# A graph network kernel: joining edge features and edge ends into rows in the first stage

## What is computed

```python
edge_index = jnp.stack([src, dst])
x = _layernorm(x + gat(x, edge_index, ...))        # three attention layers with 4 heads
x = _layernorm(x + gin(x, src, dst, ...))          # sum over neighbours, then an MLP
x = _layernorm(x + dot(x, ..., src, dst))          # dot-product attention
x = _layernorm(x + edge_net(x, edge_index, edge_attr_32, ...))
```

```python
msg = jax.nn.relu(x[src] + edge_attr @ We + be)
aggr = jax.ops.segment_sum(msg, dst, num_segments=x.shape[0])
```

## Time and profile before

| | us |
|---|---|
| median of 3 runs | 5863.4 (5854.73 to 5868.62) |
| the profiled execution, its own time | 5863.81 |
| its span in the trace | 5862.1 |
| busy PE, DVE, ACT, POOL | 3511.6, 3123.5, 2625.6, 3883.7 |

### The profile page before, as it was taken

One profiled execution on the slowest core, in us unless ns is written; L12 is line 12 of the kernel. 1 busy time (PEld: TensorE's weight loads), 2 busy tenths in 40 slices (PEclk: granted clock), 3 DMA queues, 4 the chain that ended last, 5 costly groups with the idle time before them and its releaser, 6 DMA issues. The chain is left out here.

```text
span 5862.1 us, 68109 instructions
## 1 busy us (share of the span) xinstructions
PE 3511.6 (60%) x25247; PEld 2219.0 (38%) x25248; DVE 3123.5 (53%) x3383; ACT 2625.6 (45%) x4143; POOL 3883.7 (66%) x3309
## 2 busy tenths in 40 slices
PE   3211222221034699988999889997868781667764
PEld 2211111111034455555555555554433330455542
DVE  3644555554369555445555455555579992333323
ACT  1000000000023689888888789894059891222211
POOL 1888888888884577666776578773020787777772
PEclk7555555555566899999999999998989995677765
DMA  8222222222279699757997479875542332332222
GB/s 296 20 18 20 20 18 10 1 1 0 9 251 361 169 195 199 161 115 150 195 193 156 103 164 201 184 153 152 178 166 79 109 130 74 110 81 74 75 53 24
DMA packets 427191, 683.75 MB, mean 117 GB/s; under 512 B 177678, under 2 KB 272397, under 8 KB 422768
## 3 DMA queue, kind: packets, MB, share of 16 engines
q0 software_dynamic: 236096, 287.22, 31.9%
q1 hardware_dynamic: 172432, 350.48, 17.8%
q10 hardware_dynamic: 18336, 41.70, 2.1%
HBM read 540.73 MB, written 138.43 MB: 116 GB/s over the span
## 5 line engine op out<-in xcount | busy, mean ns | idle before, releaser
L330 POOL DMA_INDIRECT counts<-plcell_add,plcell_slot x806 | 1253.9, 1556 | 385.4 <-issue 223.2
L1704 POOL DMA_INDIRECT emxg<-xtab,emsrc x856 | 944.0, 1103 | 448.4 <-issue 257.8
L714 ACT ACT_TABLE_LOAD x1 | 1.3, 1283 | 1613.2 <-PE mtps L702 1613.2
L377 PE MATMUL plpsR<-plpiece,plbefore 128*128 128x500 bf16 (+1 forms) x81 | 47.1, 582 | 813.8 <-DVE plranked L507 800.6
L422 DVE TENSOR_REDUCE plnlow<-plsame 128x13 f32<-128x1664 bf16 x62 | 117.0, 1888 | 661.6 <-DMA counts<-plcell_add,plcell_slot 661.5
L1788 PE MATMUL dotbanks<-emmsg,emsame 128*128 128x96 f32 x1712 | 316.3, 344 | 237.4 <-DVE emsame L1968 230.1
L1176 ACT ACTIVATE ga1prob<-ga1psE,ga1src_fifth 128x512 f32<-128x512 f32 (+1 forms) x700 | 407.2, 680 | 81.8 <-PE ga1psE L1281 79.1
L1176 ACT ACTIVATE ga2prob<-ga2psE,ga2src_fifth 128x512 f32<-128x512 f32 (+1 forms) x700 | 407.5, 683 | 77.0 <-PE ga2psE L1281 74.1
L1176 ACT ACTIVATE ga0prob<-ga0psE,ga0src_fifth 128x512 f32<-128x512 f32 (+1 forms) x700 | 407.1, 678 | 77.7 <-PE ga0psE L1281 74.7
L1788 PEld LDWEIGHTS dotbanks<-emmsg,emsame 128*128 128x128 f32 x1712 | 287.2, 250 | 382.2 <-issue 379.5
L1281 PE MATMUL ga0psE<-ident,ga0logit 128*128 128x128 f32 x2500 | 394.5, 288 | 55.8 <-DMA ga0logit<-log_counts 32.7
(11 more groups left out here) (403 smaller groups left out, 8577.9 us busy)
## 6 DMA issues: line engine op xcount, KB each, us to landing
ga0logit<-log_counts POOLq DMA_DIRECT2D x88, 512.0 KB
ga1logit<-log_counts POOLq DMA_DIRECT2D x88, 512.0 KB
ga2logit<-log_counts POOLq DMA_DIRECT2D x88, 512.0 KB
counts<-plzeros SPq DMA_DIRECT2D x32, 1250.0 KB, 32.7
mthalf<-counts SPq DMA_DIRECT2D x50, 800.0 KB
log_counts<-mtlogs SPq DMA_DIRECT2D x25, 1600.0 KB
ginhalf<-counts SPq DMA_DIRECT2D x50, 800.0 KB
dotlogs<-log_counts ACTq DMA_DIRECT2D x25, 1600.0 KB
```

The lines of the kernel that those rows point to most:

```text
L330: nc.gpsimd.indirect_dma_start(counts[w][:, :], bass.IndirectOffsetOnAxis(ap=cell_slot[:, g % 2, j:j + 1], axis=0), cell_add[:, g % 2, j:j ...
L377: nc.tensor.matmul(psR[:, f // RANK_BANK, 0:k * BINS], before[:], piece[:, n % 2, f:f + k, :].rearrange("p t b -> p (t b)"), start=True, s ...
L714: nc.scalar.activation(logs[:, n % OUTS, q, :], ps[:, u % 3, 0:BW], ACT.Ln, bias=tiny[:, 0:1], scale=math.e).then_inc(log_made, 1)
L1704: nc.gpsimd.indirect_dma_start(xg[:, h, t, :], None, xtab[:, :], bass.IndirectOffsetOnAxis(ap=src[:, g, t:t + 1], axis=0)).then_inc(gather ...
```

## The change

In `begin`:

- The 128 spare cells of both tables are zeroed ahead of the tables, from one partition into 256 contiguous bytes.
- A tile `whole` of 3 x 13 rows of 34 words a partition is cleared by DVE. After the 54 pieces of the unused pattern, SP loads the features of one group after the other into the first 32 words of its rows. ACT copies the ends behind them. SP stores the rows to a new DRAM tensor `edges["rows"]`, which takes the place of `edges["ends"]`. A group's turn comes at every second add of table 1.
- The column lists and the slots are stored behind that loop, and the stage ends after the last rows have landed.

In `edge_scatter`: the slots of all groups of a stage are loaded once, and each group is one load of rows into one of three buffers; the feature loads, the ends' loads and the two copies are gone.

```diff
@@ begin, SP
                 for part, done in zip(counts, zeroed):
+                    sp.dma_start(part[NP * NP:NP * NP + P, :].rearrange("(p f) o -> p (f o)", p=1), zeros[0:1, 0:P]).then_inc(done, 16)
+                for part, done in zip(counts, zeroed):
                     v = part[0:NP * NP, :].rearrange("(p j f) o -> j p (f o)", p=P, f=ZF)
                     for j in range(ZEROS):
                         sp.dma_start(v[j], zeros[:]).then_inc(done, 16)
-                    sp.dma_start(part[NP * NP:NP * NP + P, :], zeros[:, 0:1]).then_inc(done, 16)
...
+                features = a["edge_attr_32"]
+                most = features[0:(P - 1) * ET, :].rearrange("(p t) k -> p t k", t=ET)
+                rest = features[(P - 1) * ET:E, :].rearrange("(p t) k -> p t k", p=1)
+
+                def load_whole(g):
+
+                    k = g % WHOLE_BUFS
+                    if g >= WHOLE_BUFS:
+                        sp.wait_ge(whole_stored[k], 16 * (g // WHOLE_BUFS))
+                    sp.dma_start(whole[0:P - 1, k, :, 0:ED], most[:, g * G:(g + 1) * G, :]).then_inc(whole_loaded[k], 16)
+                    n = min(G, EREST - g * G)
+                    if n > 0:
+                        sp.dma_start(whole[P - 1:P, k, 0:n, 0:ED], rest[:, g * G:g * G + n, :]).then_inc(whole_loaded[k], 16)
+
+                sp.wait_ge(whole_cleared, 1)
+                load_whole(0)
+                for g in range(NG):
+                    sp.wait_ge(added[1], 16 * (4 * SORTED_GROUPS + 2 * g + 1))
+                    if g + 1 < NG:
+                        load_whole(g + 1)
+                    sp.wait_ge(whole_made, g + 1)
+                    sp.dma_start(edges["rows"][:, g * G:(g + 1) * G, :], whole[:, g % WHOLE_BUFS, :, :]).then_inc(whole_stored[g % WHOLE_BUFS], 16)
+
                 sp.wait_ge(column_made, 2)
...
                 sp.wait_ge(slots_made, 1)
-                sp.dma_start(edges["ends"][:, :, :], ends[:]).then_inc(stored, 16)
                 sp.dma_start(edges["slot"][:, :], block_i[:]).then_inc(stored, 16)
-                sp.wait_ge(stored, 64)
+                sp.wait_ge(stored, 48)
+                for k in range(WHOLE_BUFS):
+                    sp.wait_ge(whole_stored[k], 16 * len(range(k, NG, WHOLE_BUFS)))
@@ begin, DVE
                 nc.vector.memset(scan[:], 0.0)
+                nc.vector.memset(whole[:], 0.0).then_inc(whole_cleared, 1)
...
-                    step(nc.vector.tensor_copy(ends[:, :, 0], local_i[:]))
+                    nc.vector.tensor_copy(ends[:, :, 0], local_i[:]).then_inc(ends_made, 1)
+                    dve.wait_ge(ends_made, 1)
@@ begin, ACT
+            @block.scalar
+            def _(act):
+                act.wait_ge(ends_made, 1)
+                for g in range(NG):
+                    k = g % WHOLE_BUFS
+                    uses = range(k, g + 1, WHOLE_BUFS)
+                    act.wait_ge(whole_loaded[k], sum(32 if n * G < EREST else 16 for n in uses))
+                    nc.scalar.activation(whole[:, k, :, ED:RW], ends[:, g * G:(g + 1) * G, :], ACT.Copy).then_inc(whole_made, 1)
@@ edge_scatter
-    STAGES = 2
+    STAGES = 3
     count = last - first
...
+    slot = ctx.enter_context(nc.sbuf_tensor(tag + "slot", [P, max(count, 1) * G], i32))
+    stage = ctx.enter_context(nc.sbuf_tensor(tag + "stage", [P, STAGES, G, RW], f32))
...
         def load(i):
 
-            g, k, m = first + i, i % STAGES, i % LISTS
-            pool.dma_start(slot[:, m, :], edges["slot"][:, g * G:(g + 1) * G]).then_inc(list_loaded[m], 16)
-            pool.dma_start(ends[:, m, :, :], edges["ends"][:, g * G:(g + 1) * G, :]).then_inc(list_loaded[m], 16)
-            rows = feat[:, k, :, :].rearrange("p t k -> p (t k)")
+            k, g = i % STAGES, first + i
             if i >= STAGES:
-                pool.wait_ge(staged, 2 * (i - STAGES + 1))
-            pool.dma_start(rows[0:P - 1, :], most[:, g * G * ED:(g + 1) * G * ED]).then_inc(feat_loaded[k], 16)
-            n = min(G, EREST - g * G)
-            if n > 0:
-                pool.dma_start(rows[P - 1:P, 0:n * ED], rest[:, g * G * ED:(g * G + n) * ED]).then_inc(feat_loaded[k], 16)
-
+                pool.wait_ge(scattered[k], 16 * G * (i // STAGES))
+            pool.dma_start(stage[:, k, :, :], edges["rows"][:, g * G:(g + 1) * G, :]).then_inc(rows_loaded[k], 16)
+
+        pool.dma_start(slot[:], edges["slot"][:, first * G:last * G]).then_inc(slots_loaded, 16)
         load(0)
+        pool.wait_ge(slots_loaded, 16)
         for i in range(count):
...
-            nc.gpsimd.tensor_copy(stage[:, k, :, 0:ED], feat[:, k, :, :]).then_inc(staged, 1)
-            nc.gpsimd.tensor_copy(stage[:, k, :, ED:RW], ends[:, m, :, :]).then_inc(staged, 1)
-            pool.wait_ge(staged, 2 * i + 2)
+            pool.wait_ge(rows_loaded[k], 16 * (i // STAGES + 1))
```

More of the change, by code:

```diff
@@ L58 @@
 HI_BITS = 9
+WHOLE_BUFS = 3
 ZF = 5000
@@ L120, in program @@
         halves_rows = [c[0:NP * NP, :].rearrange("(r c) o -> r (c o)", c=NP) for c in counts]
-        edges = {"slot": nc.dram_tensor("edge_slot", [P, ET], i32), "ends": nc.dram_tensor("edge_ends", [P, ET, 2], f32),
+        edges = {"slot": nc.dram_tensor("edge_slot", [P, ET], i32), "rows": nc.dram_tensor("edge_rows", [P, ET, RW], f32),
                  "column": nc.dram_tensor("tile_column", [T_CHUNKS * P, 1], i32), "need": nc.dram_tensor("tile_need", [T_CHUNKS * P, 1], i32),
@@ L205, in begin @@
         ends = sb("ends", [P, ET, 2])
+        whole = sb("whole", [P, WHOLE_BUFS, G, RW])
         earlier = sb("earlier", [P, P])
@@ L237, in begin @@
         zeroed = [sem(f"zeroed{w}") for w in range(2)]
+        whole_cleared, ends_made, whole_made = (sem(n) for n in ("whole_cleared", "ends_made", "whole_made"))
+        whole_loaded = [sem(f"whole_loaded{k}") for k in range(WHOLE_BUFS)]
+        whole_stored = [sem(f"whole_stored{k}") for k in range(WHOLE_BUFS)]
         cells_made, slots_ready, rows_ready, rows_free = (sem(n) for n in ("cells_made", "slots_ready", "rows_ready", "rows_free"))
@@ L661, in make_tables @@
         pieces = [(j, k) for j in range(NB) for k in range(NB)]
-        scatter, _ = edge_scatter(nc, ctx, a, edges, "mts", *TABLE_GROUPS)
+        scatter, _ = edge_scatter(nc, ctx, edges, "mts", *TABLE_GROUPS)
         with nc.Block() as block:
@@ L767, in source_rows, with edge_scatter @@
     return row_kept, len(chunks)
-def edge_scatter(nc, ctx, a, edges, tag, first, last):
-    sb = lambda n, s, d=f32: ctx.enter_context(nc.sbuf_tensor(tag + n, s, d))
-    sem = lambda n: nc.alloc_semaphore(tag + n)
-    STAGES = 2
+def edge_scatter(nc, ctx, edges, tag, first, last):
+    STAGES = 3
     count = last - first
[L778 to L786, removed]
-    def steps(pool):
[L789 to L794, removed]
+    slot = ctx.enter_context(nc.sbuf_tensor(tag + "slot", [P, max(count, 1) * G], i32))
+    stage = ctx.enter_context(nc.sbuf_tensor(tag + "stage", [P, STAGES, G, RW], f32))
+    slots_loaded = nc.alloc_semaphore(tag + "slots_loaded")
+    rows_loaded = [nc.alloc_semaphore(f"{tag}rows_loaded{k}") for k in range(STAGES)]
+    scattered = [nc.alloc_semaphore(f"{tag}scattered{k}") for k in range(STAGES)]
+    def steps(pool):
@@ L809, in steps @@
         load(0)
+        pool.wait_ge(slots_loaded, 16)
         for i in range(count):
-            k, m = i % STAGES, i % LISTS
+            k = i % STAGES
             if i + 1 < count:
                 load(i + 1)
[L814 to L817, removed]
-            nc.gpsimd.tensor_copy(stage[:, k, :, 0:ED], feat[:, k, :, :]).then_inc(staged, 1)
@@ L819, in steps @@
-            nc.gpsimd.tensor_copy(stage[:, k, :, ED:RW], ends[:, m, :, :]).then_inc(staged, 1)
-            pool.wait_ge(staged, 2 * i + 2)
+            pool.wait_ge(rows_loaded[k], 16 * (i // STAGES + 1))
             for t in range(G):
-                nc.gpsimd.indirect_dma_start(edges["sorted"][:, :], bass.IndirectOffsetOnAxis(ap=slot[:, m, t:t + 1], axis=0),
+                nc.gpsimd.indirect_dma_start(edges["sorted"][:, :], bass.IndirectOffsetOnAxis(ap=slot[:, i * G + t:i * G + t + 1], axis=0),
@@ L906, in gat_attend @@
         place = logit[:, :, :, :].rearrange("p l q c -> p (l q c)")[:, 0:NT * HEADS * WINDOWS].rearrange("p (t w) -> p t w", w=WINDOWS)
-        scatter, scatter_steps = edge_scatter(nc, ctx, a, edges, tag + "s", *LAYER_GROUPS[layer])
+        scatter, scatter_steps = edge_scatter(nc, ctx, edges, tag + "s", *LAYER_GROUPS[layer])
         project = layer > 0
```

## The result

The changed kernel takes 6182.0 us, median of 6 runs (6174.5 to 6191.2), against 5866.3 for the kernel before in as many; the ratio is 1.0536 [1.0517, 1.0554]. It is slower, as forecast, by 5.4% and not by 12.8%: the 6613 us of the forecast are 431 too many, and the range began at 6250. The profiled execution took 6181.0 us and spans 6179.2, so 317.1 us have to be found between the two spans.

What follows compares the result with a forecast made beforehand. GpSimd's queue ended counting, VectorE the tables, TensorE and ScalarE set the layers. From 5863.8 us, +765 for SP's one-engine loads, less 15 (layers) and 1 (spare cells), gave 6613; range 6250 to 6950.

Steps and rivals of the forecast that it cites:

- What ends the stage: Counting stage: SP's feature loads, each on one DMA engine, end it at 2412 in place of 1647, +765 us.
- the 53 rows: Final store's last DMA, seen on one engine at about 20 GB/s; taken as evidence that 127-row loads use one engine.
- R1: Rival, feature loads: 127 rows go over all 16 engines, the stage ends with the adds, 5848 us; chance 0.09.
- R3: Rival, feature loads: one engine, each packet costing as one of 384 B, group 31.7 us, total 7277; chance 0.04.
- R4: Rival, counting: loads spread over 16 engines but bursts delay the adds, up to 83 us, total 5931; chance 0.02.
- R2: Rival, feature loads: one engine but 1664 B packets, load 10.4 us, in the middle +75, total 5923; chance 0.04.
- The price of a packet: Feature loads on one engine: 13.1 ns per 128 B packet, 21.6 us a load, 22.3 us a group.
- The adds' share: Counting: scatter-adds' use of the loads' engine, between none (ending 2324) and full (2485); middle taken, 2405.
- Spare cells: Start of counting: zeroing them ahead of the tables saves between 0 and 3 us, taken as 1.
- The adds end near 1642: Counting stage: GpSimd's scatter-adds still end near 1642 us while the stage stretches to about 2400.
- Layers: Three attention layers: about 67 us of GpSimd's 500 go; TensorE's mask-addition waits give back 15, within 0 to 65.
- Tables and the rest: Table building and what follows the layers: 0 us; in the tables GpSimd's removed work is hidden under VectorE.

Runs made afterwards that it cites:

- e1: Changed kernel with each 127-row feature load issued as one of 112 and one of 15 rows; 5788.6 us, ratio to before 0.9871.
- e2: Changed kernel with each 127-row feature load issued as one of 122 and one of 5 rows; 5932.0 us, one run.
- e4: Changed kernel, 127-row loads into a separate tile in 1664 B pieces, joined by ScalarE's copies; 6059.1 us, one run.
- f1: e1 with the two copies a group given back to GpSimd in the edge scatter, into a tile nobody reads; 5816.0 us, ratio to before 0.9923.
- f2: e1 with three more loads a group on GpSimd's queue in the edge scatter, into a tile nothing reads; 5826.8 us, ratio to before 0.9942.
- f4: e1 with three buffers kept and both the two copies (in place) and three more loads a group on GpSimd; 5848.1 us, ratio to before 0.9988.

## Why the prediction was right and wrong

**What ends the stage: right.** One sixteenth of the engines, 128 B pieces, the load fed from ahead, and the stage ending on SP with its last store, all as read from the 53 rows and the pieces of the earlier trace rows. e1 and e2 show the cause, not only the pattern: 112 and 15 rows, nothing left of it; 122 rows, half; and the late packets of the adds count the busy engines, one and two. The Trainium skill's rule of the largest number of engines that divides the rows (page "DMA: Bandwidth & Descriptors", section "Why a DMA increments its semaphore by 16 and not by 1") agrees with all three counts, 127, 122 and 112. R1, the only way to a faster kernel, is refuted, and so are R3 and, by e1's adds, R4's price. R2's packets are refuted for this kernel; e4, which makes them, has a load faster than R2's 10.4 us and is far slower than R2's 5923, since R2 left the adds alone.

**The price of a packet: this is the step that failed.** It was put at 13.1 ns on a line between 12.4 for 96 B and 18.8 for 384 B, with 11.7 as its low bound; it is 9.5. The row at 96 B comes from a burst of 400 packets over 16 engines, 25 an engine. The view of the earlier trace rows has more lines: the busy share of the 16 engines in each slice, in tenths, and the time that the packets took:

```profile
DMA  0006235567768999841000000000000000000000
...
q1 hardware_dynamic: 400, 0.04, 25.5%
```

In the three best slices the engines are busy nine tenths of the time or more, and a packet lasts 12.2 ns (25.5% of 16 engines' 1.2 us, over 400). So the 12.4 is the price of packets one behind the other. In the long stream a packet lasts 13.0 ns (8.5% of 16 engines' 6 us, over 629), close to the 13.1 of the forecast, but the next one starts 9.5 ns after it: they overlap, which the burst doesn't show. So 11.7 was no bound from below, and the low end should have gone well under it. A group was sized at 22.3 us for 16.7, and 62 x 5.6 is 347 of the 397 us that the first stage was over. The Trainium skill's floor of about 10.5 ns (page "DMA: Bandwidth & Descriptors", section "Bandwidth") gave 6265 us, the nearer number; it too is above what the trace shows.

**The adds' share: too large.** The middle between none and full gave 81 us. Measured are 1.1 us a group, 58 in all. That is 23 more of the 397.

**Spare cells: 24 us for 1.** The seventh add starts at 113.64 against 137.46. The prediction counted what the two DMAs move, 512 bytes, and not what 128 rows of two bytes do to the stream around them; the earlier trace rows showed 81 us of waiting, and it was taken for the time of the 41 MB. A look at the rate over those 81 us would have shown the dip. It accounts for the last 25 us: the first load of features went out at 916 and not at 941. 347 + 23 + 25 is 395 of 397.

**The adds end near 1642: wrong, at no cost here.** A cover of 0.72 us an add was reckoned for bursts on all engines and never for the one that was to be kept busy. An add uses all sixteen and lands with the slowest, as the 8 late packets in after and the 16 in e2 show, so any engine kept busy reaches each of them. It was the price of e2 and e4.

**Layers: right cause, low size, and a route shown only in part.** 15 us was the share of the changes of group among 84 runs; 51.8 is what came, within the 0 to 65 given. TensorE's waits fell by 33.4 us, not by a fifth. That the gain is GpSimd's removed work is shown by the times of f1, f2 and f4; so the share by counts, which assumed that the waits lie evenly, was too small. That it all goes by way of the waits for mask additions is not shown: with the same layers they are 36.4 us in e1, 42.6 in after, 59.3 in e4 and 63.0 in e2, while the layers' times lie within 11 us. Why the layers gain more than these waits fall stays open. GpSimd is busy 450.7 us in the first 704 of the layers, against 500.4; 67 less was forecast, but the same stretch now holds more of the layer.

**Tables and the rest: right.** -3.3 and +4.8 us for 0. The copies on ScalarE average 227 ns and wait for the loads, so they cost nothing, as said:

```profile
L373 ACT ACTIVATE plwhole<-plends 128x26 f32<-128x26 f32 x62 | 14.1, 227 | 1946.2 <-DMA plwhole<-in_edge_attr_dram 1946.2
```

## What to carry to other kernels

When a DMA moves from GpSimd's queue to SP's, look at its row count first: 127 rows ran on one engine and held SP for 16 us, while 112 and 15 rows held it for two, and the split alone made a kernel 5.4% slower into one 1.3% faster. Work that keeps a single DMA engine busy is not confined to it: here each scatter-add, spread over all sixteen, landed with its share on the busy one. Joining two tiles into one that a scatter reads ties the buffer to the scatter's landing, so count the buffers anew; and write small cells as one row, not as one cell a partition.

## What the hardware showed that was not expected

- A 128 B packet on one DMA engine takes 9.5 ns in a long stream (14 GB/s), less than the short burst shows (11.7 at best), though each lasts 13.0 ns: they overlap; 1664 B packets run at 25 GB/s.
- While one engine works off 1651 packets, SP is held 15.7 to 16.9 us at its next DMA, here one of 1.6 KB; with two engines 8.3 us.
- The share of a scatter-add that falls to a busy engine, 8 of its 128 packets, starts together, 1.7 us after the other 120; with two engines busy it is 16 of 128.
- Beside one engine kept busy with 128 B packets a scatter-add comes every 2.53 us instead of 1.87; with 1664 B packets every 3.0; beside two engines, every 2.44. Beside sixteen lightly used ones, though more bytes move, every 1.90.
- Two DMAs of 128 rows of two bytes amid a stream of writes cost 24 us; two rows of 256 B cost nothing that can be seen.
